# The attention's loop over sixteen groups of heads written out, with constants for waits and addresses

## The reference

```python
qkv = x @ w_qkv.T + b_qkv                      # 32 query heads, 8 key/value heads, width 32
q, k = apply_rope(q, 0), apply_rope(k, 0)      # in the kernel the sequence is 2048 long
k, v = jnp.repeat(k, GROUP, axis=1), jnp.repeat(v, GROUP, axis=1)      # GROUP = 4
scores = jnp.einsum('bhqd,bhkd->bhqk', q, k) / math.sqrt(HEAD_DIM)
scores = jnp.where(causal, scores, -1e20)
out = jnp.einsum('bhqk,bhkd->bhqd', jax.nn.softmax(scores, axis=-1), v)
return out @ w_o.T + b_o
```

## Time and profile before

| what | value |
|---|---|
| runs | 4028.03 us median (4026.15 to 4029.23) |
| profiled execution, its own time | 4027.74 us |
| its span, first to last instruction | 4025.9 us |
| mean granted TensorE clock | 0.969 |
| attention, first to last exponential | about 790 to 3196 us |

### The profile page before, as it was taken

The page is one execution under the profiler, slowest core; times in us unless marked ns, Lnnn a source line. Parts: engine busy times, 40 slices in busy tenths (PEclk is TensorE's granted clock), DMA queues, the critical chain, the costliest instruction groups (busy, mean ns, idle before and its releaser), DMA issues. The chain is left out here.

```text
span 4025.9 us, 69672 instructions
## 1 busy us (share of the span) xinstructions
PE 3776.8 (94%) x22272; PEld 2433.5 (60%) x22272; DVE 2292.9 (57%) x3912; ACT 1626.7 (40%) x3068; POOL 1589.7 (39%) x525
## 2 busy tenths in 40 slices
PE   2889888899999999999999999999999779999999
PEld 2777777655555555555555555555555248888887
DVE  3666656676566566566566566566566144443443
ACT  2222222155555555555555555555555521010110
POOL 5222330045544544544544544545544513232322
PEclk9999999799999999999999999999999979999999
DMA  8877785411111111111111111111110243334432
GB/s 242 209 182 193 202 200 133 97 44 47 33 46 47 33 46 47 33 46 47 33 46 47 33 46 47 33 46 47 33 46 25 70 138 94 93 87 94 90 96 65
DMA packets 240124, 325.95 MB, mean 81 GB/s; under 512 B 62795, under 2 KB 139595, under 8 KB 239859
## 3 DMA queue, kind: packets, MB, share of 16 engines
q1 hardware_dynamic: 221426, 255.22, 23.7%
q0 software_dynamic: 18432, 67.12, 7.6%
HBM read 223.67 MB, written 97.52 MB: 80 GB/s over the span
## 5 line engine op out<-in xcount | busy, mean ns | idle before, releaser
L714 DVE TENSOR_REDUCE mpart<-mx_ps 128x1 f32<-128x512 f32 (+3 forms) x2560 | 1455.1, 606 | 841.4 <-PE mx_ps L769 455.3
L672 ACT ACTIVATE probs<-st_ps 128x512 f32<-128x512 f32 (+3 forms) x2560 | 1297.7, 533 | 1093.6 <-PE st_ps L798 535.7
L656 POOL TENSOR_TENSOR sums<-probs 128x2048 f32<-128x2048 f32 (+1 forms) x320 | 1182.6, 3696 | 1256.8 <-PE den_ps L827 1171.3
L795 PE MATMUL st_ps<-qs,k_score 98*128 98x512 f32 (+3 forms) x2560 | 1087.2, 428 | 31.2 <-issue 25.3
L766 PE MATMUL mx_ps<-k_max,qs 96*128 96x512 f32 (+3 forms) x2560 | 985.4, 393 | 14.5 <-POOL consts_r L647 14.1
L795 PEld LDWEIGHTS st_ps<-qs,k_score 98*128 98x128 f32 x2560 | 482.1, 189 | 814.5 <-ACT probs L672 659.6
L810 PE MATMUL o_ps<-probs,vs 128*32 128x512 f32 (+3 forms) x5120 | 606.9, 546 | 0.0
L766 PEld LDWEIGHTS mx_ps<-k_max,qs 96*128 96x128 f32 x2560 | 495.1, 195 | 48.2 <-POOL consts_r L647 14.3
L202 POOL DMA_INDIRECT hbuf<-in_tok_table,idx x128 | 194.1, 1517 | 352.3 <-ACT xn L233 231.2
L1030 POOL TENSOR_TENSOR h<-h,bb 128x1024 f32<-128x1024 f32 x32 | 105.1, 3283 | 543.2 <-DVE xn_c L1128 543.2
L386 PE MATMUL qk_ps<-x_hi,w_hi 128*128 128x512 f32 x640 | 259.7, 406 | 51.2 <-ACT rotation L245 31.8
(11 more groups left out here) (103 smaller groups left out, 3819.9 us busy)
## 6 DMA issues: line engine op xcount, KB each, us to landing
qs<-q_hi_scratch SPq DMA_DIRECT2D x128, 256.0 KB, 4.5
h_scratch<-hbuf SPq DMA_DIRECT2D x32, 512.0 KB, 3.5
q_hi_scratch<-rot_hi SPq DMA_DIRECT2D x64, 256.0 KB, 2.6
q_lo_scratch<-rot_lo SPq DMA_DIRECT2D x64, 256.0 KB, 3.3
qs<-q_lo_scratch SPq DMA_DIRECT2D x64, 256.0 KB, 5.5
o_scratch<-o_sb SPq DMA_DIRECT2D x64, 256.0 KB
o_in<-o_scratch SPq DMA_DIRECT2D x32, 512.0 KB, 4.4
o_in<-recip_scratch SPq DMA_DIRECT2D x128, 128.0 KB, 7.9
```

The source lines that it names most:

```text
L656: nc.gpsimd.tensor_tensor(sums[:, p % SUM_SLOTS, :, j * P:CT], a, b, ALU.add).then_inc(sum_done, 1)
L672: nc.scalar.activation(probs[:, s % SLOTS, h, j * P:CT], st_ps[:, u % SCORE_BANKS, 0:CT - j * P], ACT.Exp, scale=float(HD) ** -0.5).then_i ...
L714: nc.vector.tensor_reduce(mpart[:, h * TPC + t, kc:kc + 1], mx_ps[:, n % MAX_BANKS, 0:w], AX, ALU.max).then_inc(max_done, 1)
L795: mm = nc.tensor.matmul(st_ps[:, u % SCORE_BANKS, 0:w], k_score[0:M_ROW + 2, kt * P:(kt + 1) * P], qs[c][0:M_ROW + 2, h, j * P:CT], start= ...
```

## The change

`groups` becomes a Python loop that calls `group` with a number sixteen times, on all five engines. So groups 1 to 14 are written out as groups 0 and 15 were. The helper `times` and the registers are gone, every wait in the attention is for a constant, every address in the loads and stores is a constant, and SP's increments behind its waits are gone. The order of the computing instructions and of the DMAs is the same.

```diff
-        def times(eng, g, n, reg):
-            if isinstance(g, int):
-                return g * n
-            eng.reg_mul(reg, g, n)
-            return eng.snap(reg)
-
         def groups(eng, group):
 
-            group(0, True, False)
-            with eng.Fori(1, GROUPS - 1) as g:
-                group(g, False, False)
-            group(GROUPS - 1, False, True)
+            for g in range(GROUPS):
+                group(g, g == 0, g == GROUPS - 1)
...
-                    rows = q[bass.ds(g * (GROUP * HD), GROUP * HD), c * CT:(c + 1) * CT]
+                    rows = q[g * P:(g + 1) * P, c * CT:(c + 1) * CT]
...
             def store(g, c):
                 sp.wait_ge(o_copied, g * QC + c + 1)
-                pass_waits(sp, sp_passed)
-                sp.dma_start(o_dram[bass.ds(g * P, P), c * CT:(c + 1) * CT], o_sb[:, c % 2, :]
+                sp.dma_start(o_dram[g * P:(g + 1) * P, c * CT:(c + 1) * CT], o_sb[:, c % 2, :]
                              ).then_inc(stored[c % 2], 16)
...
             def group(g, first, last):
-                ring, unit = times(pe, g, NE, ring_count), times(pe, g, NU, unit_count)
-                pair = times(pe, g, PAIRS, pair_count)
+                ring, unit = g * NE, g * NU
+                pair = g * PAIRS
```

More of the change, by code:

```diff
@@ L500, in part_b @@
         o_copied, den_copied = sem("o_copied"), sem("den_copied")
-        sp_passed = sem("sp_passed_b")
         stored = [sem(f"stored{s}") for s in range(2)]
@@ L507, in part_b @@
         block = ctx.enter_context(nc.Block())
-        def times(eng, g, n, reg):
-            if isinstance(g, int):
-                return g * n
-            eng.reg_mul(reg, g, n)
-            return eng.snap(reg)
-        def groups(eng, group):
-            group(0, True, False)
-            with eng.Fori(1, GROUPS - 1) as g:
-                group(g, False, False)
-            group(GROUPS - 1, False, True)
-        def is_first(g):
-            return isinstance(g, int) and g == 0
+        def groups(eng, group):
+            for g in range(GROUPS):
+                group(g, g == 0, g == GROUPS - 1)
         @block.sync
@@ L537, in load_k @@
                     sp.dma_start(dst[r * HD:(r + 1) * HD, c * CT:(c + 1) * CT].bitcast(F32),
-                                 k[bass.ds(g * HD, HD), c * CT:(c + 1) * CT]).then_inc(loaded[c], 16)
+                                 k[g * HD:(g + 1) * HD, c * CT:(c + 1) * CT]).then_inc(loaded[c], 16)
             def load_v(g, c):
                 sp.dma_start(vs[:, c * TPC:(c + 1) * TPC, :],
-                             v_dram[bass.ds(g, 1), :, c * TPC:(c + 1) * TPC, :].rearrange("a p t w -> (a p) t w")
+                             v_dram[g, :, c * TPC:(c + 1) * TPC, :]
                              ).then_inc(v_loaded[c], 16)
@@ L546, in store @@
                 sp.wait_ge(o_copied, g * QC + c + 1)
-                pass_waits(sp, sp_passed)
-                sp.dma_start(o_dram[bass.ds(g * P, P), c * CT:(c + 1) * CT], o_sb[:, c % 2, :]
+                sp.dma_start(o_dram[g * P:(g + 1) * P, c * CT:(c + 1) * CT], o_sb[:, c % 2, :]
                              ).then_inc(stored[c % 2], 16)
                 sp.wait_ge(den_copied, g * QC + c + 1)
-                pass_waits(sp, sp_passed)
-                sp.dma_start(den_dram[bass.ds(g * GROUP, GROUP), c * CT:(c + 1) * CT], den_sb[0:P:HD, c % 2, :]
+                sp.dma_start(den_dram[g * GROUP:(g + 1) * GROUP, c * CT:(c + 1) * CT], den_sb[0:P:HD, c % 2, :]
                              ).then_inc(stored[c % 2], 16)
@@ L644, in _ @@
         def _(pool):
-            unit_count, pair_count = pool.alloc_register("pool_unit_count"), pool.alloc_register("pool_pair_count")
             pool.wait_ge(consts, 64)
@@ L649, in group @@
             def group(g, first, last):
-                unit, pair = times(pool, g, NU, unit_count), times(pool, g, PAIRS, pair_count)
+                unit, pair = g * NU, g * PAIRS
                 for p in range(PAIRS):
@@ L661, in _ @@
         def _(act):
-            unit_count, pair_count = act.alloc_register("act_unit_count"), act.alloc_register("act_pair_count")
-            step_count = act.alloc_register("act_step_count")
             for s in range(2):
@@ L684, in group @@
             def group(g, first, last):
-                unit, pair = times(act, g, NU, unit_count), times(act, g, PAIRS, pair_count)
-                step = times(act, g, NS, step_count)
+                unit, pair = g * NU, g * PAIRS
+                step = g * NS
                 for s in range(NS):
@@ L702, in _ @@
         def _(dve):
-            ring_count = dve.alloc_register("dve_ring_count")
             dve.sem_inc(den_done, FREE)
@@ L711, in row_max @@
                 dve.wait_ge(max_ready, ring + n + 1)
-                if unit - 1 in LAST_MAX or (unit == 0 and not is_first(g)):
+                if unit - 1 in LAST_MAX or (unit == 0 and not g == 0):
                     dve.wait_ge(max_all, g * QC + c)
@@ L723, in maxima_rows @@
                 dve.wait_ge(max_ready, ring + n + 1)
-                if not (is_first(g) and c == 0):
+                if not (g == 0 and c == 0):
                     dve.wait_ge(m_rows, 32 * (g * QC + c))
@@ L738, in group @@
             def group(g, first, last):
-                ring = times(dve, g, NE, ring_count)
+                ring = g * NE
                 for s in range(NS):
@@ L750, in _ @@
         def _(pe):
-            ring_count, unit_count = pe.alloc_register("pe_ring_count"), pe.alloc_register("pe_unit_count")
-            step_count, pair_count = pe.alloc_register("pe_step_count"), pe.alloc_register("pe_pair_count")
             pe.wait_ge(consts_done, 1)
@@ L777, in give @@
                 _, what, which = ENTRIES[n]
-                if not (is_first(g) and n < MAX_BANKS):
+                if not (g == 0 and n < MAX_BANKS):
                     pe.wait_ge(max_done, ring + n - (MAX_BANKS - 1))
@@ L792, in scores @@
                     pe.wait_ge(k_score_loaded[c], LOAD * (g + 1))
-                if not (is_first(g) and u < SCORE_BANKS):
+                if not (g == 0 and u < SCORE_BANKS):
                     pe.wait_ge(exp_done, unit + u - (SCORE_BANKS - 1))
@@ L818, in denominators @@
                 pe.wait_ge(sum_done, pair + p + 1)
-                if opening and not (is_first(g) and c == 0):
+                if opening and not (g == 0 and c == 0):
                     pe.wait_ge(den_copied, g * QC + c)
@@ L834, in lagging_values @@
                     values(g, unit, k)
-                elif not is_first(g):
+                elif not g == 0:
                     values(g - 1, unit - NU, k + NS)
```

## The result

The changed kernel takes 3977.68 us (median of 4 runs, 3975.45 to 3983.40) against 4028.63 us for the kernel before beside it (4026.15 to 4031.72). The ratio is 0.9875 with a 95% interval of 0.9858 to 0.9892: 51 us or 1.25% faster. Forecast were 3979.5 us and a gain of 48 us.

The account below looks back on a forecast made before the run. PE was taken to bound the kernel, pausing at 13 attention-loop jumps. 4027.74 us less 48.35 for the jumps, all other terms 0, gave 3979.4, stated as 3979.5 us for the median; range 3975 to 3992 us.

Parts of the forecast that it names:

- What bounds the kernel: Whole kernel: PE, busy 94% of the span; in attention groups 1 to 14 it waits for issue at 13 loop jumps.
- The 13 jumps, 48.35 us: Attention loop: removing 13 jumps, with their missing code pieces, pauses and clock falls, saves 48.35 us, 3.72 us each.
- Its parts, 31.2 us idle, 15.3 us of the clock and 1.9 us of short gaps: Attention jumps' cost: PE idle, half of 30.6 us at half clock, and idle times too short for the wait view.
- The 8 us of short gaps: Straight-line attention code: upper bound for gaps the wait view misses, 112 pieces at 0.07 us.
- some 15 and no more: PE's busy time in the changed profile: forecast to fall by some 15 us and no more.
- The register instructions, taken as 0: Attention groups: removing register instructions gains 0, as PE's products cover them; bound 1.9 us over 14 groups.
- Straight-line code, taken as 0: Written-out attention: fetching about 112 pieces costs 0, each covered by PE's queued work; bounds 0 to 8 us.
- The late pieces: Rival, straight-line attention: late pieces cost 1.86 us each; every third late gives 4048 us, slower; chance 0.03.
- The turn of the group: Rival, start of each group: the pause belongs to the turn, not the jump; time unchanged at 4027.5 us; chance 0.03.
- The half gain by the other engines' fetches: Rival, attention: other engines' fetches hold PE 2.4 us in 10 of 14 groups; 4003.5 us; chance 0.05.

Follow-up runs that it names:

- the hint: Kernel before, its attention loop kept, with a prefetch hint for the jump back on PE: 3989.16 us, ratio 0.9888.
- the near jumps: Changed kernel plus a two-pass loop of one semaphore increment on PE at each of 13 group turns: 3973.23 us, ratio 0.9857.
- the groups in pairs: Kernel before with two groups in a loop pass, 6 jumps in place of 13, waits still on registers: 4006.66 us, ratio 0.9939.
- the changed kernel's second profile: Changed kernel run once more, nothing altered, as neighbour of other runs on the same chip: 3978.11 us, ratio 0.9871.
- PE's loop alone: Kernel before with the attention written out on ACT, DVE, POOL and SP, only PE keeping its loop: 4047.28 us, ratio 1.0047.
- the opposite in part C: Changed kernel with part C's loop lengthened from 2 tiles a pass to 6 (3977.32 us) or 10 (3979.54 us).

## Why the prediction was right

*What bounds the kernel.* Right. PE waits for nothing but issue in the loop, and those waits are its own jumps: with PE alone written out the gain is complete, with the other four alone there is none.

*The 13 jumps, 48.35 us.* Right in size and in cause. The profile lost 50.69 us in 14 periods. Of these 14 x (147.48 - 147.31) = 2.4 us are the registers, which leaves 48.3 us. The cause, code that has to be fetched, was read in the prediction from the count of pieces; the hint shows it (the same jumps, no pauses), the near jumps show the other side (jumps without a fetch, no pauses), and the groups in pairs show that it does not belong to the turn. The Trainium skill's rule of the page "Runtime: NRT & Kernel Launch", section "Instruction fetch mechanics", that a taken branch out of the window stalls for a fetch, holds here. Its window of two blocks does not hold for PE: a body of 1278 instructions, five pieces of 256, was kept. The skill's prices of 51 and 108 ns in "Advanced Engine Details and Errata", section "Control Flow Timing", are not to be seen in the time here: with a near jump at each turn the periods are 147.26 to 147.29 us against 147.31.

*Its parts, 31.2 us idle, 15.3 us of the clock and 1.9 us of short gaps.* The first holds: over the 14 periods PE's idle time fell by 31.29 us. Its busy time fell by 19.40 us. Of that 2.2 us are the registers: the kernel with registers and no jump has the idle time of the changed one (1.02 us) and 2.2 us more busy time (2063.55 against 2061.36 us in the changed kernel's second profile). So the clock was worth 17.2 us, more than the half of 30.6 us that I took, and why it is more than half, no run tells. The 1.9 us of gaps too short for the wait view are not there; the wait view had it all. The 8 us of short gaps at the upper end of the range were worked out from them and rest on nothing, so that end was too wide, and the wrong split did not show in the total because the whole 48.35 us came from ACT's copies. Over the whole page PE's busy time fell by 18.0 us, and by 15.5 to the changed kernel's second profile (3761.3 us), where some 15 and no more were forecast.

The mean price of 3.72 us hides two: some 2.2 to 2.9 us after the five jumps of the kernel before without a fall of the clock, and up to 6.8, in PE's loop alone, with 10 us of it. The spread of the runs goes with this. Beside the four kernels of the first series the kernel before varied from 4016 to 4054 us, with a granted clock of 0.971 in the fastest run and 0.960 in the slowest, and PE's loop alone from 4038 to 4065; each of the kernels without missing code on PE's way stayed within 8 us. Only one execution of the kernel before and one of PE's loop alone were profiled, so it is likely, but not shown, that the falls behind the jumps make the spread.

*The register instructions, taken as 0.* Slightly off: they are worth 0.16 to 0.17 us a period, 2.2 to 2.4 us in all. The bound I gave was 1.9 us. The stretch from second to third copy, which no constant-form group of the kernel before showed at full work, has 0.06 us of it (43.99 against 43.93, all from the traces), and 0.10 us (60.13 against 60.03) is in the stretch that I had bounded by 0.08. For the same reason one sign missed: the copies lie 147.31 us apart, where I had put them at 147.4 to 147.6. Nor are the registers' costs PE's: with PE alone on registers the period without a jump is 147.31 us (2940.59 to 3087.90, first copies of groups 14 and 15), and with the other four alone on registers it is 147.52.

*Straight-line code, taken as 0.* Right. No wait for issue is left, the granted clock is 1.00 over groups 1 to 14, and PE's fetches came down to 135 pieces where 137 were forecast.

*Rivals.* The late pieces did not occur: 126 pieces were fetched during the attention (790 to 3200 us), and PE's wait view has no wait for issue in that stretch. The turn of the group fell with the pairs. The half gain by the other engines' fetches did not come; their own jumps were worth 2.0 us together.

## What to carry to other kernels

Look at the engine that bounds the kernel for waits that no engine and no DMA ends, and count them: if there are as many as a loop has jumps, and the fetch queue's pieces crowd there, the body is probably larger than what the engine holds. Then write the loop out, or shorten the body below that size (not run in the attention here, only the opposite in part C); a hint to fetch the head ahead brought four fifths of the gain without larger code (4032.75 to 3989.16 us, where writing out PE's loop gave 3979.37), but it costs once where the loop ends. A loop whose body is held, or one on an engine with slack, may stay.

## What the runs showed of the hardware

- PE kept a loop body of 1278 instructions between passes and did not keep one of 2130.
- A jump of PE to code that is not held pauses it by 1.6 to 2.3 us in the attention, in the kernel before often with a second pause of up to 1.1 us some 5 us later, and by 0.5 to 0.9 us in part C. That PE's longer queue of ready products covers more of the fetch in part C is my reading and was not tested.
- A pause of 2 us on a busy PE can cost 6.8 us, by 10.2 us at half clock behind it.
- A prefetch hint for a jump that is not taken cost as much as a dear jump: 4.3 us of pause and 6.3 us of time, once at the loop's end.
- Straight-line code of some 32,000 PE instructions in the attention (2015 a group) was fetched without one visible gap.
